# Second graph layer's output projection: waits for rows by group, normalisation on ScalarE, row sums on GpSimd, bias as a product

## The reference, cut to what matters

```python
def _layernorm(x, axis=-1, eps=1e-05):
    m = jnp.mean(x, axis=axis, keepdims=True)
    v = jnp.var(x, axis=axis, keepdims=True)
    return (x - m) / jnp.sqrt(v + eps)
...
def _L1_gnn_ref(h, src, dst, W_qkv, b_qkv, W_out, b_out):
...
    h_new = jax.ops.segment_sum(msg, dst, num_segments=n)
    h_out = jnp.transpose(h_new, (0, 2, 1)).reshape(n, DIM)
    return (h_out + h) @ W_out + b_out
...
x = x + _L1_gnn_ref(_layernorm(x, axis=-1), src, dst, ...)
```

## Time and profile before

| | us |
|---|---|
| median of three executions | 2245.12 (2243.38 to 2246.44) |
| the profiled execution, its own time | 2249.73 |
| span of the trace in it | 2248.0 |
| busy in the span: PE / DVE / POOL / ACT | 1836.3 / 1618.0 / 1139.5 / 1059.4 |
| `attention_out`, from the first transfer of L2128 to that of L2241 | 1941.2 to 2008.4 |

### The profile page before, as it was taken

How to read it: one execution, slowest core, us unless ns; L and a number is a source line. 1 busy time by engine, 2 the same in 40 slices (tenths; PEclk the granted TensorE clock), 3 DMA queues, 4 the chain that set the end, 5 groups by cost and what they waited for, 6 DMA issues and landing times. The chain is left out here.

```text
span 2248.0 us, 44454 instructions
## 1 busy us (share of the span) xinstructions
PE 1836.3 (82%) x10896; PEld 1609.4 (72%) x10897; DVE 1618.0 (72%) x2925; ACT 1059.4 (47%) x2312; POOL 1139.5 (51%) x1155
## 2 busy tenths in 40 slices
PE   4699999999999998289748788888888888442898
PEld 3499999999999887289736566666666666331898
DVE  5488888888888646335457588888787887596565
ACT  1677777777777464034211544445444442010343
POOL 0476666666666213724443777767676774120200
PEclk7799999999999988589869799999999998685999
DMA  3443333333333131333145766666565663100000
GB/s 96 135 117 108 108 107 105 105 107 105 107 105 106 32 91 61 131 96 122 61 139 175 198 187 184 178 175 177 164 181 166 178 178 105 59 3 26 27 23 24
DMA packets 124317, 255.89 MB, mean 114 GB/s; under 512 B 23429, under 2 KB 68886, under 8 KB 124183
## 3 DMA queue, kind: packets, MB, share of 16 engines
q0 software_dynamic: 61792, 186.60, 28.7%
q1 hardware_dynamic: 61974, 66.65, 9.9%
q10 hardware_dynamic: 416, 1.18, 0.2%
HBM read 221.93 MB, written 34.24 MB: 114 GB/s over the span
## 5 line engine op out<-in xcount | busy, mean ns | idle before, releaser
L317 POOL DMA_INDIRECT e_rows<-h_table,e_idx x440 | 456.2, 1037 | 212.8 <-issue 107.2
L1902 POOL DMA_INDIRECT a_rows<-kv_table,a_idx x440 | 459.6, 1045 | 189.7 <-issue 147.5
L1979 PE MATMUL a_q<-q,a_spread 128*128 x880 | 254.4, 440 | 9.6 <-ACT a_spread L1953 5.9
L617 PE MATMUL e_w<-w2h,e_hidl 128*128 128x256 f32 x880 | 247.8, 304 | 2.9 <-DVE e_msg L702 2.9
L587 PE MATMUL e_agg<-e_msg,e_hot 128*128 128x256 f32 x880 | 246.8, 403 | 0.0
L618 PE MATMUL e_w<-w2l,e_hidh 128*128 128x256 f32 x880 | 226.7, 280 | 0.0
L2003 PE MATMUL a_agg<-a_rows,x 128*128 128x264 f32 x880 | 225.0, 401 | 0.0
L1979 PEld LDWEIGHTS a_q<-q,a_spread 128*128 128x128 f32 x880 | 182.9, 216 | 44.0 <-issue 12.8
L702 DVE TENSOR_TENSOR e_msg<-e_w,e_rows 128x1024 f32<-128x1024 f32 x110 | 134.7, 1225 | 94.0 <-PE e_w L621 94.0
L1921 ACT ACTIVATE a_apart<-iota_n,dst_rel 128x128 f32<-128x128 f32 x440 | 140.7, 392 | 104.0 <-PE a_agg L2003 103.5
L2003 PEld LDWEIGHTS a_agg<-a_rows,x 128*128 128x128 f32 x880 | 167.9, 200 | 24.4
(11 more groups left out here) (422 smaller groups left out, 4496.0 us busy)
## 6 DMA issues: line engine op xcount, KB each, us to landing
e_ea<-in_eaT SPq DMA_DIRECT2D x220, 64.0 KB
m_rows<-expert_rows SPq DMA_DIRECT2D x32, 272.0 KB, 2.8
e_rows<-h_table,e_idx POOLq DMA_INDIRECT x440
a_rows<-kv_table,a_idx POOLq DMA_INDIRECT x440, 3.7
q_ab<-expert_out SPq DMA_DIRECT2D x50, 128.0 KB, 3.3
kv_table<-q_kv SPq DMA_DIRECT2D x25, 256.0 KB, 2.2
u_stage<-in_m_w SPq DMA_DIRECT2D x16, 256.0 KB
x<-in_x SPq DMA_DIRECT2D x1, 3200.0 KB, 13.6
```

Source lines behind the costliest of these rows:

```text
L317: c.nc.gpsimd.indirect_dma_start(out=rows[:, g.slot8, j, :], out_offset=None, in_=table, in_offset=bass.IndirectOffsetOnAxis(ap=idx[:, g.s ...
L617: mm(w, hidl[:, g.slot, cols[k]], w2h[:, k, :], start=(k == 0), stop=False)
L1902: nc.gpsimd.indirect_dma_start(out=rows[:, g.slot * IG + j, 0:2 * D], out_offset=None, in_=c.kv_dram, in_offset=bass.IndirectOffsetOnAxis( ...
L1979: last = mm(qp[g.pair][:, j * D:(j + 1) * D], spread[:, g.pair, j, :], window(c.q, wins[j // CT]), start=True, stop=True)
```

## The change

Only `attention_out` is changed. The five transfers stay as they are. ScalarE waits for a group at that group's first normalisation, VectorE at its first add into `x`; nobody waits for all five. The normalisation of a window becomes one ScalarE instruction, `scale * x + bias` with the inverse deviation as scale and a shift as bias; VectorE works out the shifts of all 25 windows (minus mean times inverse deviation) in one small instruction at the start. The row sum moves from VectorE to GpSimd. GpSimd's bias add goes; in its place TensorE begins each window's sum with a product of a 128 x 128 matrix whose entries are all 1/128 and the bias, held once in each of the 128 partitions. VectorE keeps the division, the add into `x` and the statistics. All steps are written out, without loops, and the PSUM tiles get four banks each instead of two. ScalarE's list has the normalisation three windows ahead of the copy's step and the copy one ahead.

```diff
--- before.py
+++ after.py
@@ -2113,14 +2113,19 @@
     with ExitStack() as s:
         w, b = c.o_w, c.o_b
         rden = c.sb("o_rden", [P, NW, H], F32, s)
+        shifts = c.sb("o_shifts", [P, NW], F32, s)
+        share = c.sb("o_share", [P, P], F32, s)
         hc = c.sb("o_hc", [P, GT, D], F32, s)
         sc = c.sb("o_sc", [P, GT, D], F32, s)
         tok = c.sb("o_tok", [P, GT, D], F32, s)
         xT = c.sb("o_xT", [P, GT, KC, P], F32, s)
-        tp, op = ([c.ps(f"o_{n}{b}", [P, 512], F32, s) for b in range(2)] for n in ("tp", "op"))
-        names = ("chain", "scaled", "hc", "transposed", "xT", "rows", "added", "x", "dgate", "agate", "pgate", "tok")
-        s_d, s_sc, s_hc, s_t, s_xT, s_r, s_add, s_x, s_dg, s_ag, s_pg, s_tok = (c.sem("o_" + n) for n in names)
+        tp, op = ([c.ps(f"o_{n}{b}", [P, 512], F32, s) for b in range(4)] for n in ("tp", "op"))
+        names = ("chain", "scaled", "hc", "transposed", "xT", "rows", "x", "dgate", "agate", "pgate", "tok", "shifts", "share")
+        s_d, s_sc, s_hc, s_t, s_xT, s_r, s_x, s_dg, s_ag, s_pg, s_tok, s_sh, s_one = (c.sem("o_" + n) for n in names)
         s_back = [c.sem(f"o_back{n}") for n in range(NG)]
+        by_chunk = lambda t: t[:, 0:D].rearrange("p (k n) -> p k n", k=KC)
+        inside = lambda t: 0 <= t < NW
+        steps = range(-4, NW + 2)
         with nc.Block() as block:
             @block.sync
             def _(sp):
@@ -2129,41 +2134,41 @@
 
             @block.gpsimd
             def _(pool):
-                for g in range(NG):
-                    pool.wait_ge(s_back[g], 16)
-
-                def step(at):
-                    t = at(0)
-                    if real(t):
-
-                        need(pool, s_pg, (s_add, t.n), (s_tok, t.n + 1))
-                        nc.gpsimd.tensor_tensor(window(c.x, t.n), window(c.x, t.n), b[:, :], ALU.add).then_inc(s_add, 1)
-                rounds(pool, step, 0, 0, Window)
+                nc.gpsimd.memset(share[:, :], 1.0 / P).then_inc(s_one, 1)
+                for t in range(NW):
+                    need(pool, s_pg, (s_sc, t + 1), (s_tok, t + 1), (s_t, t - GT + 1))
+                    nc.gpsimd.tensor_tensor(hc[:, t % GT, :], sc[:, t % GT, :], tok[:, t % GT, :], ALU.add).then_inc(s_hc, 1)
 
             @block.tensor
             def _(pe):
-                def step(at):
-                    t = at(1)
-                    if real(t):
-                        need(pe, None, (s_hc, t.n + 1), (s_xT, t.free), own=True)
-                        transpose_window(nc, tp[t.bank][:, 0:D].rearrange("p (k n) -> p k n", k=KC), hc[:, t.slot, :], c.ident).then_inc(s_t, 1)
-                    t = at(0)
-                    if real(t):
-                        need(pe, None, (s_xT, t.n + 1), (s_x, t.free), own=True)
+                mm = nc.tensor.matmul
+                pe.wait_ge(s_one, 1)
+                for r in steps:
+                    t = r + 1
+                    if inside(t):
+                        need(pe, None, (s_hc, t + 1), (s_xT, t - 3), own=True)
+                        transpose_window(nc, by_chunk(tp[t % 4]), hc[:, t % GT, :], c.ident).then_inc(s_t, 1)
+                    t = r
+                    if inside(t):
+                        need(pe, None, (s_xT, t + 1), (s_x, t - 3), own=True)
+                        mm(op[t % 4][:, 0:D], share[:, :], b[:, :], start=True, stop=False)
                         for k in range(KC):
-                            last = nc.tensor.matmul(op[t.bank][:, 0:D], xT[:, t.slot, k, :], w[:, k, :], start=(k == 0), stop=(k == KC - 1))
+                            last = mm(op[t % 4][:, 0:D], xT[:, t % GT, k, :], w[:, k, :], start=False, stop=(k == KC - 1))
                         last.then_inc(s_r, 1)
-                rounds(pe, step, 1, 0, Window)
 
             @block.scalar
             def _(act):
-                def step(at):
-                    t = at(1)
-                    if real(t):
-
-                        need(act, s_ag, (s_t, t.n + 1), (s_r, t.n - GT + 1))
-                        nc.scalar.copy(xT[:, t.slot, :, :], tp[t.bank][:, 0:D].rearrange("p (k n) -> p k n", k=KC)).then_inc(s_xT, 1)
-                rounds(act, step, 1, 0, Window)
+                act.wait_ge(s_sh, 1)
+                for r in steps:
+                    t = r + 3
+                    if inside(t):
+                        need(act, s_ag, (s_hc, t - GT + 1), *([(s_back[t // GT], 16)] if t % GT == 0 else []))
+                        nc.scalar.activation(tok[:, t % GT, :], window(c.x, t), ACT.Identity, bias=shifts[:, t:t + 1], scale=c.norm.rstd[:, t:t + 1]).then_inc(s_tok, 1)
+                    t = r + 1
+                    if inside(t):
+
+                        need(act, s_ag, (s_t, t + 1), (s_r, t - GT + 1))
+                        nc.scalar.copy(xT[:, t % GT, :, :], by_chunk(tp[t % 4])).then_inc(s_xT, 1)
                 c.norm.root(act)
 
             @block.vector
@@ -2171,34 +2176,25 @@
                 v = nc.vector
                 link = Chain(dve, s_d)
 
+                v.scalar_tensor_tensor(shifts[:, :], c.norm.mv[:, :, 0], -1.0, c.norm.rstd[:, :], ALU.mult, ALU.mult).then_inc(s_sh, 1)
                 link(v.tensor_scalar(rden[:, :, :], c.agg[:, :, D:D + H], 1e-30, None, ALU.max))
                 link(v.reciprocal(rden[:, :, :], rden[:, :, :]))
-                for g in range(NG):
-                    dve.wait_ge(s_back[g], 16)
-
-                def step(at):
-                    t = at(3)
-                    if real(t):
-
-                        need(dve, s_dg, (s_hc, t.n - GT + 1))
-                        c.norm.one(t.n, tok[:, t.slot, :]).then_inc(s_tok, 1)
-                        v.tensor_tensor(sc[:, t.slot, :].rearrange("p (d h) -> p d h", h=H),
-                                        c.agg[:, bass.ds(t.n, 1), 0:D].rearrange("p a (h d) -> p (a d) h", h=H),
-                                        rden[:, bass.ds(t.n, 1), :].broadcast_to([P, DH, H]), ALU.mult).then_inc(s_sc, 1)
-                    t = at(-1)
-                    if real(t):
-                        need(dve, s_dg, (s_r, t.n + 1), (s_add, t.n + 1))
-                        v.tensor_tensor(window(c.x, t.n), window(c.x, t.n), op[t.bank][:, 0:D], ALU.add).then_inc(s_x, 1)
-                    t = at(2)
-                    if real(t):
-
-                        need(dve, s_dg, (s_sc, t.n + 1), (s_tok, t.n + 1), (s_t, t.n - GT + 1))
-                        v.tensor_tensor(hc[:, t.slot, :], sc[:, t.slot, :], tok[:, t.slot, :], ALU.add).then_inc(s_hc, 1)
-                    t = at(-2)
-                    if real(t):
-                        need(dve, s_dg, (s_x, t.n + 1))
-                        c.norm.observe(t.n)
-                rounds(dve, step, 3, 2, Window)
+                for r in steps:
+                    t = r + 3
+                    if inside(t):
+
+                        need(dve, s_dg, (s_hc, t - GT + 1))
+                        v.tensor_tensor(sc[:, t % GT, :].rearrange("p (d h) -> p d h", h=H),
+                                        c.agg[:, t, 0:D].rearrange("p (h d) -> p d h", h=H),
+                                        rden[:, t:t + 1, :].broadcast_to([P, DH, H]), ALU.mult).then_inc(s_sc, 1)
+                    t = r - 1
+                    if inside(t):
+                        need(dve, s_dg, (s_r, t + 1), (s_tok, t + 1), *([(s_back[t // GT], 16)] if t % GT == 0 else []))
+                        v.tensor_tensor(window(c.x, t), window(c.x, t), op[t % 4][:, 0:D], ALU.add).then_inc(s_x, 1)
+                    t = r - 2
+                    if inside(t):
+                        need(dve, s_dg, (s_x, t + 1))
+                        c.norm.observe(t)
                 c.norm.finish(dve)
```

## The result

The changed kernel took 2229.21 us (median of nine executions, 2223.44 to 2237.89), the kernel before beside it 2247.1 (nine, 2243.23 to 2251.64). The ratio, which is that of the means, is 0.9926, 95% interval 0.9909 to 0.9942: 0.74% faster, 16.7 us by the means and 17.9 by the medians. The forecast was 2229.7 us and a gain of 15.4.

A forecast was written before the change was run, and what follows sets the result against it. VectorE was taken to bound attention_out, 1.98 us a window. First product 1948.3, half clock until 1953.5, 23.3 x 1.52 = 35.4, end 3.95: next stage at 1993.0, gain 15.4; 2245.1 - 15.4 = 2229.7 us, range 2226.5 to 2238.5.

The forecast's parts named there:

- Waiting by group: Start of attention_out: window 0 needs only the first landing, 1945.6 instead of 1953.0, 7.4 us earlier; no later group waited for.
- TensorE as the pace: Loop of attention_out: with the bias product TensorE sets the pace, 1.52 us a window, 2.99 at half clock.
- The clock: TensorE in attention_out starts at half clock and rises 5.2 us after the first product, costing 1.7 slow windows.
- The sum: Whole of attention_out: the next stage begins at 1993.0 instead of 2008.4, gain 15.4 us, kernel 2229.7 us.
- VectorE with GpSimd: Loop of attention_out: division and GpSimd's row sum in turn make a cycle of 1.29 us, below TensorE's 1.52.
- Rival A: Loop of attention_out: row-sum work shed by VectorE returns as waiting, 1.67 us a window, 2233 us; chance 0.16.
- Rivals B, C: attention_out: B, half clock throughout, 18.9 us slower, 2264, chance 0.04; C, transfers land together, gain only 8.0, 2237, chance 0.04.
- Writing out: attention_out without loops: taken as 0, with 6.4 us of idle from code fetching as upper bound.
- rival D: TensorE in attention_out: handovers and code fetching open holes, 6.4 us and as much by waits; 2242 us; chance 0.03.

The follow-up runs named there:

- e_norm_on_vector: The changed kernel with the normalisation put back on VectorE and the row sum left on GpSimd; stage 51.1 us against 51.3, window 1.59 us.
- after_again: The changed kernel measured once more, with no edit; ratio to the kernel before 0.9929, stage 50.0 us.
- x_inverse_in_psum: x_both with the inverse denominators in PSUM instead of SBUF; ratio to the kernel before 0.9909, stage 41.9 us.
- x_bias_single: The changed kernel with the bias product in one record instead of two; stage 45.0 us against 51.3, window 1.33 us.
- x_both: x_bias_single plus 36 single-record products on TensorE ahead of the first transpose; ratio to the kernel before 0.9897, stage 43.2 us.
- x_warm: The changed kernel with ten unused products on TensorE ahead of the first transpose; stage 49.8 us against 51.3.

## Why the prediction was right, step by step

- *Waiting by group.* Forecast 7.4 us; undone, it cost 7.9. The first landing came where the rows of before had it, and no later group was waited for.
- *TensorE as the pace.* Forecast 1.52 at full clock, from 0.22 and six records of 0.215; measured 1.515. Adding a product added 0.43, taking half of one away shortened the window until another bound held.
- *The clock.* Forecast 5.2 us after the first product, measured 4.9. This was luck as much as reading: in `e_norm_on_vector` it was 2.2 and in `after_again` 2.3. The range allowed for it (a rise at once was its low end), and each microsecond is worth only 0.5.
- *The sum.* A stage of 51.8 (1993.0 - 1941.2) was forecast, 51.3 measured. That the median lies only 0.5 us from the forecast is luck on top of that: the median of the kernel before, from which the forecast started, is 2.0 higher over nine executions than over three, and the gain is 1.3 (means) to 2.5 (medians) more than forecast. Of that the stage shows 0.5.
- *VectorE with GpSimd.* Forecast 1.29, hidden under 1.52; measured 1.33, once the cover was gone. The terms were off and made up for each other: GpSimd's add takes 0.73 beside VectorE, not 0.79; the division ends 0.40 after it, not 0.45; the handover back to GpSimd takes 0.20, not 0.05.
- *Rival A* (the shed work returns as waiting) did not come about: VectorE idled before each add. But the prediction did not ask what each move off VectorE is worth by itself; with TensorE at 1.52 only one of them is a saving. The Trainium skill's page "Perfetto Trace Analysis", section "Optimizing Scalar/DVE Operations", doubts moves between GpSimd and VectorE. Here the row sum's move was indeed worth nothing, but for another reason: VectorE with the sum needs 1.51, TensorE 1.52. With the normalisation on VectorE too, the same move is worth 6.3 us (57.4 to 51.1).
- *Rivals B, C.* The clock rose, or was up already, in every trace of the study; the first landing stayed well ahead of the last.
- *Writing out.* Costed at nothing, and nothing showed in the windows of after, where VectorE idles before the adds. Single holes of some 0.3 us stand in four of the other kernels: one on VectorE marked "issue" in `x_inverse_in_psum`, and one GpSimd add that starts late in each of `x_bias_single`, `x_both` and `e_norm_on_vector`, with one window of 1.61, 1.63 and 1.89. That is far from the 6.4 us of rival D. What makes them stays open; loops around the new steps were not tried.

## What to carry to other kernels

Add up each engine's issue distances per tile, not its durations: the largest sum is the pace, and two moves off the same engine save only down to the next engine's sum. A product with a constant matrix can be the better way to add a bias even where it makes TensorE the pace (here by 2.2 us), and is cheaper still in one record. Where GpSimd works beside VectorE, try letting VectorE's two-tensor instructions take one operand from PSUM; here the division then no longer waited.

## What the runs showed of the hardware that was not expected

- For one and the same kernel, the clock rose 4.9 us after the first product in one execution and 2.3 in another, with TensorE busy throughout both; the stage moved by 1.3 us with it.
- The clock survived a pause between the warm-up products and the first transpose, of 2.1 us in `x_warm` and 1.1 in `x_both`. In `x_inverse_in_psum` it read 0.50 from about 1.4 to 4.8 us into the stage while the same products ran, and was back before the first transpose. How much TensorE had done in the stage before was not varied.
- In the three kernels with products ahead of the first transpose, the first landing came later, with the first normalisation at 5.1 to 5.4 us into the stage against 4.1 to 4.6 in the others that wait by group. Why stays open.
